# Another order of 500 steps in the fourteen middle batches of a fused attention and gating kernel

## What is computed

```
xn = layernorm(x)
s  = talking_heads_attention(xn)      # 16 heads of 16; the logits are mixed over the heads
                                      # (Wpre), softmax, mixed again (Wpost), times V, Wout
g  = silu(ffn(xn))                    # two layers; each: shift tokens, q/k/v of 8 heads of 64,
                                      # l2norm and rotary, attention in a window of 128 and the
                                      # one before it, wo, + x, layernorm, gelu-gated MLP, + x
x  = x + s * g
```

## Time and profile before

| | |
|---|---|
| median of 3 runs | 5136.95 us (5134.96 to 5141.85) |
| the profiled execution's own time | 5127.82 us |
| its span, first to last instruction | 5126.0 us |
| granted TensorE clock, mean | 0.996 |
| PE busy | 4968.1 us (97%) |
| DVE, ACT, POOL busy | 3403.0 (66%), 3111.0 (61%), 2884.7 us (56%) |

### The profile page before, as it was taken

How to read it: one execution, slowest core, us unless ns; L and a number is a source line. 1 busy time by engine, 2 the same in 40 slices (tenths; PEclk the granted TensorE clock), 3 DMA queues, 4 the chain that set the end, 5 groups by cost and what they waited for, 6 DMA issues and landing times. The chain is left out here.

```text
span 5126.0 us, 184535 instructions
## 1 busy us (share of the span) xinstructions
PE 4968.1 (97%) x76184; PEld 4078.3 (80%) x76184; DVE 3403.0 (66%) x8316; ACT 3111.0 (61%) x8075; POOL 2884.7 (56%) x2500
## 2 busy tenths in 40 slices
PE   6999999999999999999999999999999999999998
PEld 5787888878878788788787877878788788878887
DVE  6557676676766667666676666767667676676765
ACT  4566655666655666556665566565566655666655
POOL 4547555465655656555565555655546555465653
PEclk9999999999999999999999999999999999999999
DMA  2312112121111211112111111112112122121111
GB/s 85 119 51 86 46 74 75 42 69 70 54 74 46 74 58 54 74 46 78 54 54 74 66 62 50 64 64 74 54 61 71 46 74 71 45 70 63 57 62 30
DMA packets 61215, 325.84 MB, mean 64 GB/s; under 512 B 6368, under 2 KB 23776, under 8 KB 43488
## 3 DMA queue, kind: packets, MB, share of 16 engines
q1 hardware_dynamic: 49632, 297.26, 15.4%
q0 software_dynamic: 10752, 16.78, 1.7%
HBM read 288.33 MB, written 34.08 MB: 63 GB/s over the span
## 5 line engine op out<-in xcount | busy, mean ns | idle before, releaser
L1575 POOL TENSOR_TENSOR q_lo<-q_mix,q_hi 128x512 fp32r<-128x512 f32 x512 | 662.1, 1293 | 863.0 <-ACT q_hi L1041 862.7
L1054 ACT ACTIVATE probs<-bank_S,neg_max 128x512 f32<-128x512 f32 x1024 | 699.0, 684 | 725.2 <-DVE neg_max L1307 639.1
L759 PE MATMUL bank_S<-k_hi,q_lo 128*128 128x512 f32 x2048 | 879.4, 429 | 35.3 <-POOL q_lo L1575 21.6
L1307 DVE TENSOR_REDUCE neg_max<-bank_S 128x1 f32<-128x512 f32 x1024 | 697.0, 687 | 295.8 <-PE bank_S L761 290.7
L761 PE MATMUL bank_S<-k_hi,q_hi 128*128 128x512 f32 x2048 | 806.3, 394 | 0.0
L760 PE MATMUL bank_S<-k_lo,q_hi 128*128 128x512 f32 x2048 | 805.6, 393 | 0.0
L1570 POOL TENSOR_TENSOR q_mix<-q_rope,w_pre 128x256 f32<-128x256 f32 x1024 | 633.1, 646 | 43.4 <-POOL q_lo L1575 0.9
L776 PEld LDWEIGHTS bank_M<-mixer_n,probs 64*64 64x64 f32 x32768 | 530.5, 135 | 155.9 <-issue 135.8
L776 PE MATMUL bank_M<-mixer_n,probs 64*64 64x64 f32 x32768 | 597.9, 221 | 8.1 <-DVE o_locT_lo L1416 3.4
L1601 POOL TENSOR_TENSOR l_probs<-l_probs,l_inv 128x1024 f32<-128x1024 f32 (+1 forms) x256 | 430.2, 1688 | 273.6 <-DVE l_inv L1410 272.8
L1586 POOL TENSOR_TENSOR inv_norms<-norms_c,minus_half 128x16 f32<-128x16 f32 x128 | 418.1, 3266 | 251.2 <-DVE norms_c L1344 249.2
(11 more groups left out here) (157 smaller groups left out, 11372.0 us busy)
## 6 DMA issues: line engine op xcount, KB each, us to landing
w_qkv_hi<-split_qkv SPq DMA_DIRECT2D x30, 1536.0 KB, 9.7
w_qkv_lo<-split_qkv SPq DMA_DIRECT2D x30, 1536.0 KB, 6.4
w_hi<-split SPq DMA_DIRECT2D x30, 1408.0 KB, 6.1
w_lo<-split SPq DMA_DIRECT2D x30, 1408.0 KB, 6.1
w_hi<-split SPq DMA_DIRECT2D x30, 768.0 KB, 5.4
w_lo<-split SPq DMA_DIRECT2D x30, 768.0 KB, 7.2
w_o_hi<-split_o SPq DMA_DIRECT2D x30, 512.0 KB, 3.7
w_o_lo<-split_o SPq DMA_DIRECT2D x30, 512.0 KB, 4.7
```

Of the source, the lines that this page charges most:

```text
L759: mm(bank[k][:], q_lo[q], k_hi[:, s, :], start=(s == 0), stop=False)
L1054: fn(probs[:, n % PB, :], bank[k][:], ACT.Exp, bias=neg_max[:, n % 2:n % 2 + 1], accum_out=row_sum[:, n % 4:n % 4 + 1]).then_inc(emptied[k ...
L1307: v.tensor_reduce(neg_max[:, n % 2:n % 2 + 1], bank[k][:], AX.X, ALU.max, negate=True)\
L1575: g.tensor_tensor(q_lo[:, c % QB], q_mix[:], q_hi[:, c % QB].bitcast(F32), ALU.subtract)\
```

## The change

`ORDER` is replaced by another order of the same steps. No step is added or taken away, and `FIRST_ORDER` and `LAST_ORDER` stay. One wait is added for PE, in batch 1 alone. The first row of the table and the wait, as the diff shows them (the other 31 rows of the table differ in the same way):

```diff
-expand.0 part.0 expand.1 qkv.0.0 join.0.0 part.1 scores.0 scores.1 qkv.0.1 scores.2 expand.2 bound q_turn.0.0 mixers.0
+expand.0 part.0 expand.1 qkv.0.0 part.1 join.0.0 scores.0 qkv.0.1 scores.1 scores.2 bound expand.2 q_turn.0.0 mixers.0
...
             def x_turn(step, l):
                 stream_ready(pe, now, l)
+                if now.b == 1 and not l:
+                    pe.wait_ge(bias_folded, LAYERS)
                 for c in range(KC):
```

More of the change, by code:

```diff
@@ L157 @@
-hide.1.1 scores.63 mix.30 mixers.31 up.1.2 up.1.3 mix.31 scale hide.1.2 hide.1.3 up.1.4 values.7 x_turn.0 up.1.5
-project.3 hide.1.5 hide.1.4 talk_k talk_q down.1.0 down.1.1 down.1.2 talk_v down.1.3
+expand.0 part.0 expand.1 qkv.0.0 part.1 join.0.0 scores.0 qkv.0.1 scores.1 scores.2 bound expand.2 q_turn.0.0 mixers.0
+join.0.1 k_turn.0.0 part.2 qkv.0.2 q_turn.0.1 k_turn.0.1 expand.3 scores.3 scores.4 part.3 expand.4 join.0.2 mixers.1
+mix.0 qkv.0.3 part.4 mix.1 scores.5 k_turn.0.2 mixers.2 join.0.3 q_turn.0.2 scores.6 mix.2 q_turn.0.3 sigmoid.0
@@ new lines @@
+expand.5 part.5 scores.7 k_turn.0.3 scores.8 mixers.3 local_scores.0.0 scores.9 expand.6 mix.3 weigh.0.0 part.6
+local_scores.0.1 scores.10 expand.7 mixers.4 sigmoid.1 part.7 values.0 weigh.0.1 local_scores.0.2 p_turn.0.0 scores.11
+mix.4 weigh.0.2 scores.12 p_turn.0.1 mixers.5 sigmoid.2 local_values.0.0 expand.8 part.8 scores.13 scores.14 mix.5
+expand.9 sigmoid.3 p_turn.0.2 local_values.0.1 mixers.6 silu gated part.9 expand.10 local_scores.0.3 scores.15
+scores.16 mix.6 mixers.7 out_proj.0.0 weigh.0.3 local_scores.0.4 scores.17 mix.7 local_scores.0.5 weigh.0.4 weigh.0.5
@@ new lines @@
+p_turn.0.3 local_values.0.2 values.1 mixers.8 scores.18 local_values.0.3 part.10 p_turn.0.4 expand.11 local_scores.0.6
+mix.8 scores.19 out_proj.0.1 weigh.0.6 local_values.0.4 part.11 p_turn.0.5 mixers.9 expand.12 local_scores.0.7
+local_values.0.5 p_turn.0.6 weigh.0.7 scores.20 scores.21 mix.9 part.12 out_proj.0.2 local_values.0.6 p_turn.0.7
+mixers.10 scores.22 local_values.0.7 expand.13 part.13 scores.23 out_proj.0.3 store mix.10 half_turn.0 expand.14
+mixers.11 scores.24 project.0 shift_turn.0 mix.11 scores.25 scores.26 mixers.12 values.2 h_scale.0 part.14 scores.27
@@ new lines @@
+mix.12 mixers.13 expand.15 h_turn.0 part.15 scores.28 scores.29 mix.13 mixers.14 up.0.0 hide.0.0 up.0.1 hide.0.1
+up.0.2 up.0.3 expand.16 hide.0.2 hide.0.3 part.16 up.0.4 up.0.5 hide.0.5 hide.0.4 scores.30 expand.17 mix.14 part.17
+scores.31 expand.18 scores.32 down.0.0 part.18 down.0.1 mixers.15 down.0.2 down.0.3 expand.19 mix.15 x_turn.1
+scores.33 mixers.16 qkv.1.0 join.1.0 qkv.1.1 values.3 k_turn.1.0 join.1.1 q_turn.1.0 qkv.1.2 part.19 q_turn.1.1
+join.1.2 expand.20 scores.34 k_turn.1.1 qkv.1.3 scores.35 mix.16 mixers.17 q_turn.1.2 scores.36 k_turn.1.2 join.1.3
@@ new lines @@
+part.20 scores.37 expand.21 mix.17 q_turn.1.3 scores.38 k_turn.1.3 mixers.18 part.21 project.1 expand.22
+local_scores.1.0 scores.39 mix.18 weigh.1.0 part.22 mixers.19 local_scores.1.1 scores.40 scores.41 p_turn.1.0 mix.19
+weigh.1.1 mixers.20 local_scores.1.2 expand.23 scores.42 values.4 local_values.1.0 part.23 expand.24 weigh.1.2
+p_turn.1.1 scores.43 mix.20 mixers.21 local_scores.1.3 scores.44 scores.45 mix.21 p_turn.1.2 weigh.1.3
+local_values.1.1 mixers.22 local_scores.1.4 part.24 expand.25 scores.46 scores.47 mix.22 local_scores.1.5 out_proj.1.0
@@ new lines @@
+local_values.1.2 weigh.1.4 mixers.23 part.25 scores.48 p_turn.1.3 scores.49 mix.23 weigh.1.5 expand.26
+local_scores.1.6 p_turn.1.4 local_values.1.3 part.26 mixers.24 weigh.1.6 expand.27 values.5 scores.50 out_proj.1.1
+local_values.1.4 p_turn.1.5 part.27 mix.24 expand.28 local_scores.1.7 local_values.1.5 weigh.1.7 p_turn.1.6 scores.51
+scores.52 out_proj.1.2 local_values.1.6 part.28 p_turn.1.7 project.2 mixers.25 local_values.1.7 expand.29 part.29
+scores.53 out_proj.1.3 mixers.26 mix.25 half_turn.1 scores.54 scores.55 expand.30 mix.26 mixers.27 scores.56 part.30
@@ L159 @@
+shift_turn.1 mix.27 expand.31 scores.57 scores.58 values.6 mixers.28 part.31 h_scale.1 scores.59 mix.28 mixers.29
+h_turn.1 scores.60 scores.61 mix.29 norm up.1.0 up.1.1 mixers.30 hide.1.0 hide.1.1 scores.62 scores.63 mix.30 scale
+mixers.31 up.1.2 up.1.3 hide.1.2 hide.1.3 mix.31 up.1.4 values.7 x_turn.0 up.1.5 hide.1.5 hide.1.4 project.3 talk_k
+talk_q down.1.0 down.1.1 talk_v down.1.2 down.1.3
 """
```

## The result

The changed kernel takes 5196.96 us (median of four runs, 5193.73 to 5203.28), the kernel before 5135.95 in the same session (5134.77 to 5141.85). The ratio is 1.012, with a 95% interval of 1.0108 to 1.0133. The prediction was 5119 us with a range of 5095 to 5146, so it was wrong in sign. The profiled execution took 5197.73 us, 69.9 more than that of before.

A forecast was written before the change was run, and what follows sets the result against it. PE, busy 97% of the span, was taken to bound the kernel. Gains of 3.7 us less losses of 2.4 gave 1.3 us a batch, 18 us in all, hence 5119 us, with a range of 5095 to 5146.

The forecast's parts named there:

- `mix.11`: PE waits here for M0, since the store was taken to land 6.1 us after issue: loss 1.3 us a batch.
- rival 3: Slower by the store's landing alone, stretched beside weight loads; 5193 us at a landing of 11.4 us; chance 0.11.
- `scores.2`: PE's wait here for q_lo goes, as q_lo now stands ahead of `join.0.0`: gain 1.1 us a batch.
- `k_turn.1.1`: PE's wait here for `join.1.1` is covered by `scores.34`, now put between: gain 1.2 us a batch.
- `k_turn.0.3`: PE's wait here for `mix.2`'s bank M1 is covered by `scores.7`, now between: gain 0.6 us a batch.
- `mix.5`: PE's wait here for M1, held up by DVE's `sigmoid.2`, is covered by `scores.14`: gain 0.3 us a batch.
- `k_turn.1.0`: Now ahead of `q_turn.1.0`, which no longer covers part of its wait for `join.1.0`: loss 0.2 us a batch.
- `mix.2`: Less PE work covers the 2.7 us chain to its second mixing weight: loss 0.4 us a batch.
- `p_turn.0.3`: PE wants this transpose sooner than the weights from `weigh.0.3` are there: loss 0.2 us a batch.
- `local_values.0.5`: Only `local_scores.0.7` is left between it and `p_turn.0.5`, whose copies take longer: loss 0.3 us a batch.
- the store would be hidden anyway: Loss at `mix.11` only 0.25 us, net 2.35 us a batch, 5104 us; chance 0.25.
- the gains would be used up by small new waits: Waits not followed add 1.3 us a batch, so the net is nothing, 5137 us; chance 0.19.

The follow-up runs named there:

- experiment 4: Changed kernel, with layer 0's loads of `w_1_lo` and `w_2` issued only behind `mix.11` in all batches but the first: 5139.99 us.
- 7: Changed kernel, with only layer 0's load of `w_1_lo` delayed until `mix.11` has filled its bank, in all batches but the first: 5193.96 us.
- experiment 9: Changed kernel, with only layer 0's two loads of `w_2` delayed until `mix.11` has filled its bank, in all batches but the first: 5138.77 us.
- Number 5: Changed kernel with one step moved, `part.13` behind `half_turn.0` instead of ahead of the store: 5102.65 us.
- 6: Kernel before with the store behind `out_proj.0.3`, `project.0` behind `scores.24` and `part.13` behind `local_values.0.7`: 5254.93 us.
- number 1: Changed kernel with only the store put back, right behind `part.9`: 5107.49 us.
- experiment 10: Changed kernel with 22 extra matmuls ahead of `mix.11` in batches 1 to 14, while PE waits anyway: 5180.97 us.
- Experiment 8: Changed kernel with the store behind `weigh.0.5` and `q_turn.1.0` ahead of `k_turn.1.0` again: 5081.24 us.
- number 2: Kernel before with two steps moved, the store behind `out_proj.0.3` and `project.0` behind `scores.24`: 5141.39 us.

## Why the prediction was wrong

**The step that failed** is the duration in the term for `mix.11`: "lands 6.1 us later". All sixteen rows behind that 6.1 were taken where no weights are loaded: in the trace no packet of SP's queue moves during any of them. The other times of the term were right to 0.2 us (issue at +3.73 for +3.9, `scores.24` at +5.53 for +5.54, M0 wanted at +9.3 for +9.2). With 11.1 in place of 6.1 the same sum gives a loss of 6.3, and the traces show 6.1 (6.29 against 0.17). That is rival 3, to which I gave 0.11. It was the case that the text itself described best: it named the loads, their place and a comparable transfer of 11.4 us. What I set against it, that a copy from memory to memory may suffer more than a store, rested on no row. The trace of before could have priced it, too: of the sixteen copies behind the 11.4, the one of batch 0 has no load beside it and lands in 4.2 us, and the other fifteen, 0.5 to 1.3 us behind two loads of weights, in 10.1 to 11.9. Experiments 4, 7 and 9 show that the loads of `w_2` make the landing, and 5 and 6 that `part.13` ahead of the store brings it beside them.

The Trainium skill says that inside each DMA engine the queues of the two kinds of issue are served in turn (DMA: Bandwidth & Descriptors, SWDGE vs HWDGE vs iDMA). The trace agrees for a part of the landing. These are the packets of SP's queue (q1) and of POOL's (q0) in the changed kernel, batch 7: from the store's issue to 2415, from there to 2419, and to 2422.5 (number of packets, MB, share of the 16 DMA engines):

```profile
q1 hardware_dynamic: 200, 1.58, 98.0%
...
q1 hardware_dynamic: 183, 0.95, 70.5%
q0 software_dynamic: 173, 0.18, 32.9%
...
q0 software_dynamic: 492, 0.85, 98.0%
```

In the middle stretch the two queues start about as many packets each, but POOL's carry 1 KB and SP's 5 KB, so the store gets a sixth of the bytes. In the first, 4 us long, none of POOL's packets starts. In batches 2 to 14 the first comes 4.5 to 4.8 us behind the store's issue, and 1.9 us behind it where no load is near (numbers 1 and 4). Taking turns doesn't account for this delay of 2.7 us, which is over half of the 4.9 us by which the landing grew; its cause stays open.

**What no term held** is the low clock. The stall of 6 us at `mix.11` is followed by matmuls at half speed, which made the steps behind it 2.0 us a batch longer (2.38 against 0.39), 28 us of the kernel. In experiment 10, where PE is busy for most of the stall, these 2.0 us are gone. My rival 3 had 5193 us from a landing of 11.4; with 11.1 it gives 1.3 - 5.0 = -3.7 a batch, 5189 us. The clock makes that worse by 2.0 a batch, and the rest of the order makes it better.

**The other terms**, in us a batch:

| term | predicted | measured |
|---|---|---|
| `scores.2` | +1.1 | +1.10 |
| `k_turn.1.1` | +1.2 | +1.19 |
| `k_turn.0.3` | +0.6 | +0.63 |
| `mix.5` | +0.3 | +0.42 |
| `project.0` beside full-height matmuls | +0.3 | +0.36 |
| `shift_turn.0` | +0.2 | +0.13 |
| `k_turn.1.0` | -0.2 | -0.36, and -0.14 at `q_turn.1.0` behind it |
| `mix.2` | -0.4 | -0.12, and -0.21 at `k_turn.0.2` |
| `p_turn.0.3` | -0.2 | none |
| `local_values.0.5` | -0.3 | none |
| `local_values.1.5` (no term) | | -0.24 |
| `mix.11` | -1.3 | -6.12 |
| low clock (no term) | | -1.99 |

All the gains came, to within 0.12 us. The small losses came out at 1.1 in all, as predicted, though not at the places predicted. Other places, each under 0.4 either way, bring a further 0.8 that I had no term for. Without the store's two rows (`mix.11` and the low clock) the new order is worth 3.5 us a batch; I had 2.6. Experiment 8 shows that to be real: its sum is 21.1 us a batch against 25.0, so 3.9 x 14 = 55 us, and the measured times differ by 57. Of the 3.9, 0.5 are from `q_turn.1.0` back in its old place.

**The rivals.** That the store would be hidden anyway (0.25) and that the gains would be used up by small new waits (0.19) are both ruled out, the second by the table above. The signs named in advance for q_lo and `k_turn` came, and so did the one for rival 3, a wait for s_tok above 2.5 us: it is 7.0 at DVE and 6.1 at PE. The wait of `mix` for its mixing weights, 0.3 to 0.4, doesn't show among PE's waits.

**What I got wrong on the way.** Four expectations failed by more than a few us: number 2, because I took the list's neighbour for the time of issue; numbers 1 and 4, because I left out what the moved piece costs at its new place (1.34 us on POOL, and the loads beside `h_turn.0`); and number 10, whose clock came back while only half of the time did. Number 5's time held, but its landing (9.5 us for 6 to 7.5) failed, and number 10's text has the low clock wholly behind the stall, where it begins within it.

## What to carry to other kernels

A transfer's duration belongs to its place: take it from a transfer that runs beside what will run beside it, or carry the whole span between the two as the likely case. When a DMA issue is moved, look at what stands ahead of it on the issuing queue and at what is queued within a landing's time behind it, on every queue; and charge the issue itself (1.34 us here) to what stands behind it. A stall of PE of this length costs more than itself: look at the granted clock behind it (2.0 us behind 6.1 here).

## What the hardware showed that I had not expected

- A store of 512 KB issued by POOL lands in 6.2 us alone (number 1) and in 7.2 us with a load of 1408 KB issued on SP's queue 2.6 us ahead of it (9). With two loads of 768 KB issued 0.4 us behind it, it lands in 10.5 us (7), and with all three in 11.1 us. It lands in 9.5 us when the load of 1408 KB is issued 1.5 us behind it and the other two 4.5 us (5).
- The store slows the others too: in the changed kernel the load of the next input that POOL issues 3.3 us behind the store lands in 9.1 us in the median. With the same loads of weights and the store elsewhere (number 8) it lands in 6.1.
- The granted clock fell to 0.50 within each stall of some 6 us, 0.9 to 4.1 us before its end, and was there for 6.8 us (10.2 in batch 1), so for 3.3 to 6.1 us behind the stall. In experiment 4 it was there for 3.4 us, seven times in the middle batches, each time after PE had idled for 2.0 to 3.1 us, and in experiment 9 eight times, again after 2.0 to 3.1 us.
